# Two folded LoRA layers on one core: the second bias's row sums and two h products placed behind the first batch's first product, four bias additions and one operand split reordered

## The reference, cut to what matters

```python
x = x + (x @ W.T + b + 2 * (x @ A0[i0]) @ B0[i0])        # x: (8, 256, 1024), rank 16, 32 slots
x = x + (x @ base_W.T + base_b + (x @ A1[i1].T) @ B1[i1].T)
```

## Time and profile before

| | |
|---|---|
| median of 3 runs | 281.93 us (281.27 to 282.66) |
| the profiled execution's own time | 282.09 us |
| its span, first to last instruction | 280.5 us |
| TensorE busy | 275.7 us, 98% of the span |
| VectorE busy | 214.6 us, 77% |
| ScalarE busy | 101.6 us, 36% |
| granted TensorE clock, mean | 1.000 |

### The profile page before, as it was taken

How to read it: one execution, slowest core, us unless ns; L and a number is a source line. 1 busy time by engine, 2 the same in 40 slices (tenths; PEclk the granted TensorE clock), 3 DMA queues, 4 the chain that set the end, 5 groups by cost and what they waited for, 6 DMA issues and landing times.

```text
span 280.5 us, 3865 instructions
## 1 busy us (share of the span) xinstructions
PE 275.7 (98%) x1321; PEld 224.8 (80%) x1321; DVE 214.6 (77%) x321; ACT 101.6 (36%) x141; POOL 21.7 (8%) x48
## 2 busy tenths in 40 slices
PE   8999999999999999999999999999999999999995
PEld 6888887888888885888877888888877888888885
DVE  5789999999899699898982875875772865875413
ACT  4665464352964575404231223132221223132000
POOL 3333200401002001001000000000000000000000
DMA  7997000200376200293701713702802302303003
GB/s 231 395 419 294 29 1 0 60 19 0 108 268 266 110 2 9 77 348 133 241 22 65 240 56 121 232 15 114 245 1 78 132 0 112 95 2 128 22 0 150
DMA packets 13112, 33.93 MB, mean 121 GB/s; under 512 B 2165, under 2 KB 2421, under 8 KB 13094
## 3 DMA queue, kind: packets, MB, share of 16 engines
q1 hardware_dynamic: 12066, 31.60, 31.8%
q0 software_dynamic: 1024, 2.10, 2.4%
q10 hardware_dynamic: 4, 0.00, 0.0%
HBM read 22.09 MB, written 11.60 MB: 120 GB/s over the span
## 4 chain that ended last, share of the span: by engine, by line
PE 60%; DVE 2%; issue 0%
PE bank L1305 18%; PE bank L1306 18%; PE bank L1307 18%; PE bank L1337 3%; PE bank L1312 3%; DVE ops L739 1%; PE bank L1370 0%; PE bank L1371 0%; PE bank L1369 0%; DVE ops L806 0%; DVE g_all L763 0%; DVE raw_a L808 0%; DVE raw_a L936 0%; PE bank L1372 0%; DVE aa L862 0%
## 5 line engine op out<-in xcount | busy, mean ns | idle before, releaser
L1305 PE MATMUL bank<-ops,late 128*128 128x512 f32 x192 | 75.1, 391 | 0.0
L1306 PE MATMUL bank<-ops,late 128*128 128x512 f32 x192 | 74.8, 389 | 0.0
L1307 PE MATMUL bank<-ops,late 128*128 128x512 f32 x192 | 74.7, 389 | 0.0
L1145 PE MATMUL bank<-ops 128*128 128x512 f32 x112 | 43.6, 389 | 0.0
L1146 PE MATMUL bank<-ops 128*128 128x512 f32 x112 | 43.6, 389 | 0.0
L1305 PEld LDWEIGHTS bank<-ops,late 128*128 128x128 f32 x192 | 36.0, 188 | 8.7 <-issue 1.2
L1307 PEld LDWEIGHTS bank<-ops,late 128*128 128x128 f32 x192 | 36.0, 188 | 7.6
L1306 PEld LDWEIGHTS bank<-ops,late 128*128 128x128 f32 x192 | 36.0, 188 | 7.4
L1141 PE MATMUL bank<-ops 128*128 128x512 f32 x112 | 40.7, 398 | 0.2 <-issue 0.2
L536 ACT CAST late<-rows 128x512 fp32r<-128x512 f32 x24 | 14.7, 621 | 54.6 <-DVE rows L834 29.6
L1141 PEld LDWEIGHTS bank<-ops 128*128 128x128 f32 x112 | 21.4, 192 | 5.1 <-issue 0.4
(11 more groups left out here) (177 smaller groups left out, 397.8 us busy)
## 6 DMA issues: line engine op xcount, KB each, us to landing
out<-raw_a SPq DMA_DIRECT2D x27, 256.0 KB, 2.3
raw_a<-xT SPq DMA_DIRECT2D x10, 512.0 KB, 6.6
a<-rb_rows SPq DMA_DIRECT2D x8, 392.0 KB
x_mid<-xT SPq DMA_DIRECT2D x6, 512.0 KB, 6.2
raw_b<-W SPq DMA_DIRECT2D x2, 1024.0 KB, 15.6
rb_rows<-b_hl SPq DMA_DIRECT2D x3, 512.0 KB
rb_rows<-late SPq DMA_DIRECT2D x3, 512.0 KB
raw_b<-V SPq DMA_DIRECT2D x4, 256.0 KB, 4.3
```

What stands on the lines that cost most here:

```text
L1145: mm(bank[:, :], left(u, 0, k, m), op_k(v, 1, k), start=False, stop=False, skip_group_check=on_top)
L1305: mm(bank[:, :], hi, t_op(t, 0, k), start=(start and k == 0), stop=False, skip_group_check=not start)
L1306: mm(bank[:, :], hi, t_op(t, 1, k), start=False, stop=False, skip_group_check=not start)
L1307: last = mm(bank[:, :], lo, t_op(t, 0, k), start=False, stop=(k == KH - 1), skip_group_check=not start)
```

## The change

On VectorE the first four `bias_add` steps, with their waits for the bias and for vt3, move from the place ahead of low("us4") to the place of the other four, behind L996. On ScalarE high("t1") goes ahead of the copy c_hl[0], on VectorE low("t1") ahead of c_hl[1]. On TensorE the two products for the sums of the bias row and the h products of batches 0 and 1 go from the place ahead of the batch loop to behind p1(0). No instruction is added or removed, and the amount of work is the same.

```diff
             for n in range(KH):
                 high_d21(n)
+            act.wait_ge(summed["t1"], KH)
+            high("t1")
             act.wait_ge(c_summed, 1)
             nc.scalar.copy(c_hl[0], Z[0:NH * CT, :]).then_inc(c_split, 1)
-            act.wait_ge(summed["t1"], KH)
-            high("t1")
             keep_p1(0)
...
             nc.vector.tensor_tensor(b0_sum[:, :], b0_raw[:, 0:KH], b0_raw[:, KH:KT], ALU.add).then_inc(b0_summed, 1)
-            dve.wait_ge(bias1_landed, DMA)
-            dve.wait_ge(summed["vt3"], 1)
-            bias_first(0)
-            bias_first(1)
             dve.wait_ge(m1_kept, KH)
             low("us4")
...
-            bias_first(2)
-            bias_first(3)
+            dve.wait_ge(bias1_landed, DMA)
+            dve.wait_ge(summed["vt3"], 1)
+            for k in range(KH):
+                bias_first(k)
             dve.wait_ge(lo[SLOT["v11"]], filled("v11", KH))
             dve.wait_ge(bias_step, 2 * KH)
             combine("vt2", "v11", "vt3", ALU.subtract)
...
+            low("t1")
             dve.wait_ge(c_split, 1)
             nc.vector.tensor_tensor(c_hl[1], Z[0:NH * CT, :], c_hl[0], ALU.subtract).then_inc(c_split, 1)
-            low("t1")
             make_u2(0)
...
-            pe.wait_ge(bias_step, 2 * KT)
-            pe.wait_ge(lo[SLOT["d22"]], filled("d22", KH))
-            pe.wait_ge(summed["t1"], KH)
-            for j in range(NH):
-                last = mm(Z[j * CT:(j + 1) * CT, :], ones_b[:, 0:CT], bias_sum[:, j * CW:(j + 1) * CW],
-                          start=True, stop=True)
-            last.then_inc(c_summed, 1)
-            h_product(0)
-            h_product(1)
             for b in range(B):
                 p1(b)
+                if b == 0:
+
+                    pe.wait_ge(bias_step, 2 * KT)
+                    pe.wait_ge(lo[SLOT["d22"]], filled("d22", KH))
+                    pe.wait_ge(summed["t1"], KH)
+                    for j in range(NH):
+                        last = mm(Z[j * CT:(j + 1) * CT, :], ones_b[:, 0:CT], bias_sum[:, j * CW:(j + 1) * CW],
+                                  start=True, stop=True)
+                    last.then_inc(c_summed, 1)
+                    h_product(0)
+                    h_product(1)
                 p6(b)
```

## The result

| | before | after |
|---|---|---|
| median, 22 runs each | 282.07 us (281.21 to 282.92) | 282.86 us (282.42 to 284.20) |
| ratio, 95% interval | | 1.0037 (1.0029 to 1.0045) |
| profiled execution | 282.09 us | 283.30 us |
| its span | 280.5 us | 281.7 us |

The changed kernel is slower, by 0.8 us as the difference of the medians and by 1.04 us as the ratio (0.0037 x 282.07). Forecast were 282.6 us and +0.6 us. Both are inside the 0.5% that was called "no change", but with 22 runs the sign is clear. The interval of the ratio is +0.8 to +1.3 us, so the +0.5 to +0.7 us that the sum allowed was too small, while the time lies well inside the stated range.

What follows compares the result with a forecast made beforehand. TensorE, busy 98% of the span, was taken as the bound, so only its waits count. +1.15 us at the second G product less 0.55 at the h product gave +0.6, forecast 282.6 us, range 281.0 to 283.9.

Steps and rivals of the forecast that it cites:

- Part 1: VectorE, bias additions moved: 1.99 us idle ahead of low("us4"), then combine("vt2") and all behind it 1.99 us later.
- The wait at the G product: TensorE waits about 1.5 us at the second G product (L1159) for the A difference; +1.15 us in the sum.
- M3's gain: M3's first matmul on TensorE starts 0.45 us earlier, which is lost again completely at the second G product.
- Part 2: TensorE, p1(0) ahead of the sums and h products: the wait at the h product goes, 0.55 us gained.
- Part 3: ScalarE and VectorE, t1 ahead of the rows: costs nothing on TensorE; the rb issue moves from 116.81 to about 121.0.
- A: VectorE's lateness is covered, no wait arises at the second G product: -1.0 us, about 281.0; chance 0.08.
- B: R's bounce lands late and delays the h product: +1.4 us at 2.2 us beyond the shift; chance 0.10.
- C: The rb load arrives late for its first reader: a wait of 1.8 us, 284.5 us; chance 0.07.
- D: The 1.5 us wait lowers TensorE's clock to 1.2 GHz for 24 matmuls: 5.4 us more, 288.1; chance 0.02.

Runs made afterwards that it cites:

- after_look1: The changed kernel once more, nothing altered, as a second profiled execution: 282.82 us.
- after_look2: The changed kernel once more, nothing altered, as a third profiled execution: 282.94 us.
- three_ahead: The changed kernel with three of the eight first bias additions ahead of low("us4"), five behind: 281.60 us against 281.72 before, ratio 0.9996.
- look1: The kernel before, unchanged, one more profiled execution: 281.71 us.
- look3: The kernel before, unchanged, the third of three more profiled executions: 281.62 us.
- bias_only: The kernel before with only the move of VectorE's bias additions: 283.34 us against 281.72, ratio 1.0056.
- rows_first: The changed kernel with the 64-row pieces back ahead of t1 on ScalarE and VectorE: 282.96 us against 281.61 before, ratio 1.0060.
- adiff_early: The changed kernel with the low half of the A difference moved ahead of low_r: 282.10 us against 281.72 before, ratio 1.0009.

## Why the prediction was right, point by point

**Part 1, idle time and shift: right.** Idle 1.97 us (1.99 forecast); combine("vt2") at 56.81 is 21.85 behind S, 19.79 before, a shift of 2.06 against 1.99. It ran through to L1033, 46.53 behind S against 44.46, undiminished.

**The wait at the G product: right, and a little undersized as a loss.** The wait was 1.34 us against 1.5. Measured from S it is the 1.20 by which the G product starts later, plus 0.59 that M3 had gained, less 0.45 that TensorE lost on the way, at the S product (both below). The start against before, which is what counts, moved by 1.20 where 1.05 stood in the sum: 0.08 more shift, and a hand-over from VectorE to TensorE of 0.15 (82.17 to 82.32) where 0.08 was taken. The slow start behind it was 0.08 to 0.15, against 0.10. Together +1.3 against +1.15.

**M3's gain was one sample too.** M3 started 9.53 us behind S here, against 10.12 before, but 10.08 and 10.15 in after_look1 and after_look2, where TensorE's own sequence was the limit. So the 0.45 us is not a constant, and it was 0.59, 0.04 and -0.03 us measured from S. It didn't matter for the sum, as the forecast says: it is lost again at the G product each time. It is one reason why three_ahead missed its 1.0 us (M3 10.29 and 9.77 us behind S in its two executions, against 10.12 before); the other is the h product's gain (part 2).

**The S product's wait was missed.** TensorE came to L1266 at 68.28 and started it at 68.61, since VectorE's b1 half was as late as all else. With the slow start behind it this took 0.45 us (M3 to M6's last matmul is 36.26 us, 35.81 before). It cost nothing, because the G product's wait behind it was long enough to take it up; after_look1 does not list it.

**Part 2: the mechanism was right, the term mis-sized.** "so 0.55 us is gained" is the step that failed as a figure for the median. In the profiled pair it was even 0.68, because the sums and the h product overlap when nothing separates them: the forecast put the h product 0.96 us behind the sums, and it started 0.02 us behind them (112.89 and 112.91). But in look1 and look3 there was nothing to gain. Over the kernel before's four executions the gain is 0.25 us; the sum is then 1.20 + 0.10 - 0.25 = +1.05 us, against 1.04 by the ratio and 0.79 by the medians. Four executions, three of them on one chip, don't fix that average well, so the closeness to 1.04 is in part chance. The forecast worked from one profile and took a wait behind a chain of DMAs for a constant.

**Part 3: right by the pieces.** low("t1") ended at 117.57, the low rows at 118.16 (118.4 forecast), the rb issue came at 120.79 (121.0), the first ranks at 129.33 followed without a wait. The issue answers the earlier trace rows:

```profile
118.19 1.31 SPq L377 DMA_DIRECT2D rb_rows<-rows  x4
120.79 0.75 SPq L320 DMA_DIRECT2D a<-rb_rows  x2
```

**The rivals.** A (the lateness is covered) did not occur in any of the six executions with all additions behind (the three of the changed kernel, bias_only, rows_first, adiff_early). B's second wait did occur, but in bias_only, where the old order leaves the h product exposed: the new order is what keeps it from the changed kernel. ScalarE's first x cast came at 95.94 (96.15 forecast), and at 96.56 and 96.41 in after_look1 and after_look2, still in time, but B was nearer than it looked. The h product had 1.40 us in hand in the first execution, as forecast, and 0.30 and 0.46 us in these two, whose t_sum took 8.38 and 8.02 us instead of 6.80. (In after_look1 factors(0) ends at 112.14 and the h product starts at 112.44.) Whether B did happen in the runs that lie 1 us above the others (284.20; 284.0 twice in rows_first) is not known, as none of them was profiled.

C (rb late) did not occur. D (the clock falls behind the wait) did not: TensorE's window with the wait, busy 0.82 of 2.00 us, and the one behind it (us, busy and count of PE, PEld, DVE, ACT and POOL, granted clock, DMA share, GB/s) both have 1.00, 2.4 GHz:

```profile
81.00:83.00 2.00, 0.82 (x4) 0.63 (x4) 2.00 (x3) 2.00 (x3) 0.00 (x0) 1.00 0.80 231
83.00:85.00 2.00, 2.00 (x11) 1.65 (x10) 2.00 (x2) 1.32 (x3) 0.00 (x0) 1.00 0.50 176
```

The 24 matmuls in D's price come from no row, and nothing here tests that price.

## What to carry to other kernels

Taking work off an engine ahead of an instruction that waits for another engine brings only what that wait leaves: count the idle time that the work was filling (here 1.97 of 2.65 us), leave exactly that much in place (three additions of four), and follow the rest to the next reader with the smallest margin. Read a wait in one profile as one sample: where the chain behind it holds DMAs, look at several executions, or at what its releaser does in other kernels, before its length goes into a sum. And fix a ruler, an instruction that the change does not touch, and compare pieces from it, when two executions differ by more than the effect.

## What the runs showed of the hardware that was not expected

- The transfer of t_sum, 0.5 KB written from 128 partitions to DRAM, took 6.64 to 8.38 us from its issue to the next in 14 executions of the same code, while the pieces of the same kernel that VectorE sets repeated within 0.02 us (S to G of before and of the changed kernel). SyncE's queue stood still for it, 7.3 us in the first profile, and everything behind it in the queue is as late.
- The sums (two fp32 products of 32 columns of weights, four matmul records) and the h product's matmuls, which also use 32 columns each, run into one another when neither waits: 2.70 us for the sums and both h products, against 3.37 with a wait of which 0.45 us is idle. So 0.22 us more than the idle time was lost at that wait.
- Where the A difference released the G product (five executions), TensorE started 0.14 to 0.15 us behind VectorE's end; at M3 and at the h product of the first profile it was 0.10 and 0.06 us. The matmuls from G to M4's last took another 0.08 to 0.15 us in all behind such a wait.
